# Rank-one attention: argument products over 32 rows instead of 2, selections and averages built elsewhere, sums issued one place later

## The reference, cut to what matters

```python
x_avg = jnp.mean(x, axis=(2, 3), keepdims=True)
se_mid = jax.nn.relu(conv1x1(x_avg, se1_w, se1_b))
W_cw = jax.nn.sigmoid(conv1x1(se_mid, se2_w, se2_b))
g_x, theta_x, phi_x = (conv1x1(x, w, v).reshape(b, N) for w, v in ...)   # one row each
f = theta_x[:, :, None] * phi_x[:, None, :]
f_div_C = jax.nn.softmax(f, axis=-1)
y = jnp.einsum('bij,bj->bi', f_div_C, g_x)
return W_cw * (bn(W_w * y + W_b)) + x
```

## Time and profile before

| | us |
|---|---|
| median of 3 runs | 2866.69 (2864.36 to 2867.64) |
| the profiled execution, its own time | 2868.04 |
| its span, first to last instruction | 2866.2 |
| last stage, from its first instruction on | 2808.9 to 2866.2 |

### The profile page before, as it was taken

The page is one execution under the profiler, slowest core; times in us unless marked ns, Lnnn a source line. Parts: engine busy times, 40 slices in busy tenths (PEclk is TensorE's granted clock), DMA queues, the critical chain, the costliest instruction groups (busy, mean ns, idle before and its releaser), DMA issues. The chain is left out here.

```text
span 2866.2 us, 45891 instructions
## 1 busy us (share of the span) xinstructions
PE 2743.7 (96%) x20113; PEld 1361.1 (47%) x20113; DVE 2156.5 (75%) x1392; ACT 1663.3 (58%) x2577; POOL 74.1 (3%) x66
## 2 busy tenths in 40 slices
PE   7399999999999999999999999999799999999898
PEld 3334444444344344443444444444478888757552
DVE  5499999999999999999999999998442221224344
ACT  2467776777777777777677777766422222211253
POOL 0000000000000000000000000000431000000000
PEclk9799999999999999999999999999899999999997
DMA  1100000000001000000000000100600000200001
GB/s 69 39 25 22 23 29 9 29 29 16 29 9 35 23 15 29 22 23 29 9 29 29 16 29 10 35 5 1 194 1 0 1 1 0 84 0 1 0 1 59
DMA packets 38760, 72.26 MB, mean 25 GB/s; under 512 B 21088, under 2 KB 22048, under 8 KB 36896
## 3 DMA queue, kind: packets, MB, share of 16 engines
q1 hardware_dynamic: 38496, 69.19, 7.4%
q0 software_dynamic: 64, 0.13, 0.0%
HBM read 60.45 MB, written 8.86 MB: 24 GB/s over the span
## 5 line engine op out<-in xcount | busy, mean ns | idle before, releaser
L734 PE MATMUL l_ps<-mlp_w,W2H 128*64 128x512 f16 x8192 | 1366.4, 392 | 18.0 <-DVE mlp_w L768 18.0
L768 DVE TENSOR_TENSOR mlp_w<-words_x,words_y 128x2048 f32<-128x2048 f32 x512 | 1159.5, 2287 | 66.9 <-PE l_ps L734 66.9
L734 PE MATMUL l_ps<-mlp_w,W2L 128*64 128x512 f16 x4096 | 802.3, 388 | 0.0
L734 PEld LDWEIGHTS l_ps<-mlp_w,W2H 128*64 128x64 f16 x8192 | 455.1, 108 | 550.1 <-issue 116.4
L815 ACT ACTIVATE relu_bottom<-l_ps 128x512 f32<-128x512 f32 x1024 | 612.3, 598 | 79.4 <-PE l_ps L734 1.4
L815 ACT ACTIVATE mlp_w<-l_ps 128x512 f32<-128x512 f32 x684 | 408.8, 598 | 279.7 <-PE l_ps L734 249.8
L752 DVE SCALAR_TENSOR_TENSOR mlp_w<-relu_bottom,sign_ratio,mlp_w 128x2048 f32<-128x2048 f32 x171 | 401.4, 2348 | 7.6 <-ACT relu_bottom L815 7.6
L734 PEld LDWEIGHTS l_ps<-mlp_w,W2L 128*64 128x64 f16 x4096 | 229.0, 109 | 179.7 <-issue 0.8
L815 ACT ACTIVATE relu_top<-l_ps 128x512 f32<-128x512 f32 x340 | 203.2, 598 | 135.7 <-PE l_ps L734 120.8
L723 PE MATMUL l_ps<-y_rows,y_weights_halves 12*128 12x512 bf16 x2048 | 202.4, 385 | 12.5 <-DMA y_rows<-y_pieces 12.5
L752 DVE SCALAR_TENSOR_TENSOR relu_top<-relu_bottom,sign_ratio,relu_top 128x2048 f32<-128x2048 f32 x85 | 199.5, 2348 | 4.0 <-ACT relu_bottom L815 4.0
(11 more groups left out here) (375 smaller groups left out, 2549.3 us busy)
## 6 DMA issues: line engine op xcount, KB each, us to landing
table_pos<-pos_table SPq DMA_DIRECT2D x64, 512.0 KB, 3.8
mlp_w<-in_mlp_w SPq DMA_DIRECT2D x8, 1024.0 KB, 13.2
X<-in_x SPq DMA_DIRECT2D x8, 512.0 KB, 7.4
bias_scratch<-bias_rows SPq DMA_DIRECT2D x64, 64.0 KB, 2.0
mlp_w_hi<-bias_scratch SPq DMA_DIRECT2D x16, 256.0 KB, 3.9
out<-Q SPq DMA_DIRECT2D x16, 256.0 KB, 2.1
y_rows<-y_pieces SPq DMA_DIRECT2D x192, 12.0 KB
xn_b<-in_out_wT SPq DMA_DIRECT2D x1, 1024.0 KB, 7.9
```

What stands on the lines that cost most here:

```text
L734: last = nc.tensor.matmul(out[q][a * DH:(a + 1) * DH, :], w[:, half], h[a][:, :, k], start=False, stop=stop, tile_position=(0, a * DH))
L768: nc.vector.tensor_tensor(hw[i % 3][:, r].rearrange("p (m j) -> p m j", j=J), words_x, words_y[:, 2 * n + r].unsqueeze(1).to_broadcast([P, ...
```

## The change

- `arguments` makes its products over all 32 rows of a strip in place of two. The rows added hold zeros in both operands.
- POOL's clearing and the selection matrices move to the start of `stage_nonlocal`. They lie in a part of `K.WR` that both stages leave alone. PE and DVE need not wait for them any more.
- Of the eight averages at the end of `stage_nonlocal` the last four move to ACT's start of `stage_rank_one`; DVE's addition of them waits there.
- In the loop `columns(0)` and `replicate(0, 0)` are issued ahead of `weigh(r - 1)` of their step, and `replicate(0, 1)` ahead of the last `weigh`.

```diff
@@ stage_nonlocal
+        @block.gpsimd
+        def _(pool):
+            nc.gpsimd.memset(K.gw, 0.0).then_inc(sel, 1)
+            nc.gpsimd.memset(K.sel_q, 0.0).then_inc(sel, 1)
+            nc.gpsimd.memset(K.sel_k, 0.0).then_inc(sel, 1)
...
-            for i in range(NT * CC):
-                t, c = divmod(i, CC)
-                act.wait_ge(o_out, (B - 1) * NT * CC + i + 1)
-                act.wait_ge(mean, CC + i)
-                nc.scalar.activation(ex[2][:, 0:BANK], K.X[:, c, B - 1, t * BANK:(t + 1) * BANK], ACT.Copy,
-                                     accum_out=(K.av_b[:, c:c + 1] if t else K.av[:, c, 1:2])).then_inc(mean, 1)
+            for c in range(CC):
+                act.wait_ge(o_out, (B - 1) * NT * CC + c + 1)
+                act.wait_ge(mean, CC + c)
+                nc.scalar.activation(ex[2][:, 0:BANK], K.X[:, c, B - 1, 0:BANK], ACT.Copy, accum_out=K.av[:, c, 1:2]).then_inc(mean, 1)
@@ stage_rank_one
-        @block.gpsimd
-        def _(pool):
...
             pe.wait_ge(g_out, 1)
-            pe.wait_ge(sel, 3 + 4 * B * NT)
...
-                        last = nc.tensor.matmul(args[k % 3][:, u], keys[b][at:at + 2, jj * P:(jj + 1) * P], queries[b][at:at + 2, :],
+                        last = nc.tensor.matmul(args[k % 3][:, u], keys[b][at:at + 32, jj * P:(jj + 1) * P], queries[b][at:at + 32, :],
...
             for r in range(B * JJ):
                 arguments(r)
-                if r:
-                    weigh(r - 1)
                 if r == JJ + 1:
                     columns(0)
                 if r == JJ + 2:
                     replicate(0, 0)
+                if r:
+                    weigh(r - 1)
+            replicate(0, 1)
             weigh(B * JJ - 1)
-            replicate(0, 1)
             columns(1)
...
-            dve.wait_ge(sel, 1)
             nc.vector.tensor_copy(gw[:, :, 0:3], K.v("gtp_w", 0, 3 * CC).rearrange("p (c k) -> p c k", k=3)).then_inc(w_pad, 1)
+            dve.wait_ge(av_in, CC)
             nc.vector.tensor_tensor(av[:, :, 1], av[:, :, 1], K.av_b[:], ALU.add).then_inc(head, 1)
...
         @block.scalar
         def _(act):
+            for c in range(CC):
+                if c:
+                    act.wait_ge(av_in, c)
+                nc.scalar.activation(scaled[1], K.X[:, c, B - 1, BANK:], ACT.Copy, accum_out=K.av_b[:, c:c + 1]).then_inc(av_in, 1)
             act.wait_ge(head, 3)
```

More of the change, by code:

```diff
@@ L1404, in stage_nonlocal @@
     z = room([P, HW])
+    K.sel_q, K.sel_k, K.sel_m, K.gw = room([P, B, P]), room([P, B, P]), room([P, B * NT, P]), room([P, CC, 32])
     eT = carver(K.Q)([P, PC, HW])
@@ L1415, in stage_nonlocal @@
     z_mm, z_out, o_mm, o_out = K.sem("z_mm"), K.sem("z_out"), K.sem("nlo_mm"), K.sem("nlo_out")
-    bn, mean = K.sem("bn3_step"), K.sem("mean_sums")
+    bn, mean, sel = K.sem("bn3_step"), K.sem("mean_sums"), K.sem("selection")
     NF = 2 * B
@@ L1422, in stage_nonlocal @@
     with nc.Block() as block:
+        @block.gpsimd
[3 more added lines that the diff above has]
+            nc.gpsimd.memset(K.sel_k, 0.0).then_inc(sel, 1)
+            pool.wait_ge(sel, 3)
+            for b in range(B):
+                q, k = (w[:, b].rearrange("p (t u r) -> p t u r", t=NT, u=2) for w in (K.sel_q, K.sel_k))
+                for t in range(NT):
+                    n = 32 * (NT * b + t)
+                    nc.gpsimd.tensor_copy(q[:, t, :, 0:2], K.k("ident", n + 1, 1).unsqueeze(2).to_broadcast([P, 2, 2])).then_inc(sel, 1)
+                    nc.gpsimd.tensor_copy(k[:, :, t, 0], K.k("ident", n + 2, 1).to_broadcast([P, NT])).then_inc(sel, 1)
+                    nc.gpsimd.tensor_copy(k[:, :, t, 1], K.k("ident", 3, 1).to_broadcast([P, NT])).then_inc(sel, 1)
+            for n in range(B * NT):
+                nc.gpsimd.tensor_copy(K.sel_m[:, n], K.k("ident", 32 * n + 2, 1).to_broadcast([P, P])).then_inc(sel, 1)
+            pool.wait_ge(sel, 3 + 4 * B * NT)
         @block.tensor
@@ L1621, in stage_rank_one @@
     sums = [room([P, BANK]) for _ in range(B)]
-    sel_q, sel_k, sel_m = room([P, B, P]), room([P, B, P]), room([P, B * NT, P])
+    sel_q, sel_k, sel_m, gw = K.sel_q, K.sel_k, K.sel_m, K.gw
     out = carver(K.Q)([P, CC * B, HW])
-    gw = sb("gtp_w32", [P, CC, 32])
     mid, gate = sb("se_mid", [SE, B]), sb("gate", [P, CC, B])
@@ L1633, in stage_rank_one @@
     pps = args[1][:, 0, 0:2 * B * NT]
-    sel, w_pad, head = K.sem("selection"), K.sem("gtp_w_padded"), K.sem("r1_small")
+    w_pad, head, av_in = K.sem("gtp_w_padded"), K.sem("r1_small"), K.sem("avg_last")
     av_d, g_mm, g_out, t_mm, t_out = K.sem("avg_done"), K.sem("gtp_mm"), K.sem("gtp_out"), K.sem("rowsT_mm"), K.sem("rowsT_out")
```

## The result

The changed kernel took 2845.07 us in the median of four runs (2844.42 to 2847.83), the kernel before 2865.53 in four (2863.12 to 2867.64): ratio 0.9931, 95% interval 0.9913 to 0.9948. Measured again with five runs against 21 of the kernel before, the ratio was 0.9951 (0.9939 to 0.9964), 14 us. The profiled execution took 2844.42 us.

What follows compares the result with a forecast made beforehand. The loop was taken to be bound by PE at half clock, with DVE's chain behind it. Seam 1.0 and loop 14.3 gave 15.3 us, so 2866.69 became 2851.4; own range 2849 to 2854.5, widened with rival 1 to 2848.5 to 2857.5.

Steps and rivals of the forecast that it cites:

- Seam: Entry to the last stage: barrier opens 0.76 us sooner, DVE's copy no longer waits for POOL (0.24); together 1.0 us.
- Loop: Last stage's loop: at full clock and in the new order, the second spreading ends at 2839.32 instead of 2853.66.
- Steps of 2.01 and 2.25 in turn: Loop at full clock: steps alternate because every second one waits for an exponential to free a PSUM tile; mean 2.13 us.
- Last stage: From the loop to the end of the second spreading: 14.3 us less, with the tail behind it unchanged.
- The order: Loop: spreading no longer stands behind sums; about 2 us of the 14.3.
- the clock: Loop: products over 32 rows in four strips keep PE at 2.4 GHz instead of 1.2; 12.3 us.
- the third rival: Argument products: four strips stop overlapping with 32 rows; 2870.3 us, at half clock 2902; chance 0.02.
- rival 1: Clock still falls at the loop's head and comes back in the loop, costing 1.5 to 5 us: 2853 to 2856.5; chance 0.10.
- the second: Row count doesn't matter to the clock; only seam and new order gain, about 3.2 us in all: 2863.5; chance 0.13.
- the runs scatter by 1.7: Whole program: the scatter of runs that the forecast's own range, 2849 to 2854.5, allowed for.
- the base of the sum: Whole program: median of three runs of the kernel before, 2866.69 us, from which 15.3 was taken.
- Its reading that work over all 128 rows brings the clock back: Loop: clock returned at 2848.34 after a 128 x 128 spreading, nearly all zeros, so full-height work was taken to raise it.

Runs made afterwards that it cites:

- 32 rows alone: Kernel before with one edit, argument products over 32 rows of a strip in place of two: 2853.45 us, ratio 0.9967 (0.9955 to 0.9980).
- a kernel with two rows: Changed kernel with two-row argument products again, new seam and order kept: 2859.53 us, ratio 0.9987 (0.9979 to 0.9996).

## Why the prediction was right and wrong

Its mechanisms held, each near its size. Seam: 1.0 forecast, 1.01 found. Loop: the outputs of the second half image were walked to 29.9 us behind the first product of the row vectors (2839.35 less 2809.41) and stand at 30.23. Steps of 2.01 and 2.25 in turn were 2.07 and 2.24 (sums 1.00, not 0.93). Last stage: 14.3 forecast, 14.0 found. The order at about 2 of it was 2.1, the clock at 12.3 was 12.0 in the run of the 32 rows alone. All four strips overlap as before (1.07), so the third rival fell; the first did not occur; the second was refuted by 32 rows alone. Its own case, a kernel with two rows, was sized at 3.2 and came to 5.3 in the profile and 3.7 (1.1 to 6.0) in the ratio: the slow stretch is not always 27.3 us long.

The Trainium skill's TensorE: Matmul & The Clock Gate (section on the HAM clock gate) has the clock follow how busy PE is. These runs agree only in part. Where PE had waited, in `stage_nonlocal`, the clock fell, and with the waits filled it did not. But in the loop PE was busy throughout with 2, 8, 16 and 24 rows and got 1.2 GHz for 17 to 27 us, and with 32 rows, busy for 22.03 of 27.40 us only, it got 2.4.

What failed is the step "the runs scatter by 1.7", and with it the base of the sum, 2866.69, and the range. I took the scatter from three runs (2864.36 to 2867.64), and their median as the kernel's. Over all executions the same kernel took 2858.61 to 2867.64, and 2862.90 in the median of 21. The forecast stood on a base 3.8 us too high, and had no term for the stages ahead, in which two executions of one kernel can lie 7.1 us apart. The page of before showed dips ahead of the last stage, and I costed only the one that I meant to move; that they change from execution to execution one trace could not show. With 2862.90 as the base the same sum gives 2847.6; the changed kernel again took 2848.78, and the median of its nine runs is 2847.69. So of the 6.3 us between 2851.4 and 2845.07, 3.8 are the base and 2.5 the place of the first four runs in the changed kernel's own scatter (2844.42 to 2849.54); that both went the same way was bad luck. The profiled pair is 23.6 us apart, 15.0 of the change and 8.6 ahead of it; of the 20.5 between the first medians what goes beyond the change is put down to such scatter too.

Two slips in the working changed nothing: its own terms add up to 2848.7 to 2855.5, a little more than the range that it states, and forecast and rival 1 hold 0.85 where its last count has 0.86. Its reading that work over all 128 rows brings the clock back, nearly all zeros or not, fits seven of the eight executions in which the clock fell in the loop; with 24 rows it came back without a turning or a spreading ahead of it.

## What to carry to other kernels

Look at the granted clock beside the busy share: a loop in which PE never rests can still run at half speed, and, as here, products over a few rows can be made over whole strips at no cost in their own time (1.07 us for four), if the added rows are zeros. Each wait in which the clock falls is a term with a scatter of its own, so a forecast of less than 1% needs the scatter of the whole program, read from more than three runs, and the verdict on a part is better taken from that part's length in the profile than from the total.

## What I had not expected of the hardware

- 16 rows a strip (2.02 us for eight records), and two full strips of four, gave nothing over two rows; 24 shortened the slow stretch from 20.5 to 17.1 us (one execution each); 32 in all four removed it (five executions).
- Zeros were enough: 30 of 32 rows are zeros in both operands, and the clock read 1.00 for 27.4 us.
- The kernel before alone moved by 9.0 us (2858.61 to 2867.64) between executions; in the two that were profiled, 7.1 us apart, the stretches at 1.2 GHz ahead of the last stage account for 6.8.
